# A decoder layer on one core: inverse roots of the norms moved from VectorE to GpSimd

## The reference

```python
def l2norm(x):
    return x * jax.lax.rsqrt(jnp.sum(x * x, -1, keepdims=True) + 1e-06)      # on q and k, per head
...
def head_stats(x):
    mean = x.mean(-1)
    var = ((x - mean[..., None]) ** 2).mean(-1)
    am = jnp.abs(x).mean(-1)
    l2 = jnp.sqrt((x * x).sum(-1))
    return jnp.stack([mean, var, am, l2], -1).mean(2)
def rmsnorm(x, w):
    return x * jax.lax.rsqrt((x * x).mean(-1, keepdims=True) + EPS) * w
...
x = _layernorm(x + _L0_attn_ref(...), axis=-1)    # delta rule, convolutions, mixture of four sources, gate
x = _layernorm(x + _L0_xattn_ref(...), axis=-1)   # retention over a context
x = _layernorm(x + _L0_ffn_ref(...), axis=-1)     # eight experts, the best two of each token count
```

## Time and profile before

| | |
|---|---|
| Median of 3 runs | 513.29 us (512.7 to 514.06) |
| Span of the profiled execution, first to last instruction | 510.6 us |
| Median less that span (the profiled execution lists no time of its own beside its span) | 2.7 us |
| PE matmul busy | 401.5 us, 79% of the span |
| DVE busy | 323.2 us, 63% |
| ACT busy | 159.2 us, 31% |
| POOL busy | 39.3 us, 8%, nearly all of it before 160 us |
| DVE instructions | 1050 |

### The profile page before, as it was taken

One profiled execution on the slowest core, in us unless ns is written; L12 is line 12 of the kernel. 1 busy time (PEld: TensorE's weight loads), 2 busy tenths in 40 slices (PEclk: granted clock), 3 DMA queues, 4 the chain that ended last, 5 costly groups with the idle time before them and its releaser, 6 DMA issues.

```text
span 510.6 us, 8321 instructions
## 1 busy us (share of the span) xinstructions
PE 401.5 (79%) x2952; PEld 293.4 (57%) x2952; DVE 323.2 (63%) x1050; ACT 159.2 (31%) x267; POOL 39.3 (8%) x77
## 2 busy tenths in 40 slices
PE   1979999788973699984245689897998979887992
PEld 0647677467962699971023355565656546564672
DVE  2043464677999823368763576676897588777635
ACT  1252523512345211142021124422433244413430
POOL 7000000002980000000000000000000000000000
PEclk9989999997997555575555969999899989999997
DMA  7460201039653900000000000000020000000000
GB/s 246 105 186 1 42 0 22 1 75 296 166 145 88 119 3 3 3 2 0 1 1 27 15 21 1 0 22 0 2 62 2 21 0 21 0 0 1 22 2 21
DMA packets 48305, 22.23 MB, mean 44 GB/s; under 512 B 17768, under 2 KB 47632, under 8 KB 48016
## 3 DMA queue, kind: packets, MB, share of 16 engines
q1 hardware_dynamic: 31760, 13.40, 10.9%
q10 hardware_dynamic: 16512, 8.39, 6.0%
HBM read 18.64 MB, written 3.15 MB: 43 GB/s over the span
## 4 chain that ended last, share of the span: by engine, by line
PE 49%; DVE 31%; issue 9%; DMA 5%; ACT 3%; SPq 2%; DVEq 0%; ACTq 0%; POOL 0%
PE bank L460 9%; PE bank L493 5%; PE bank L691 5%; PE bank L699 5%; PE bank L721 5%; PE bank L733 4%; PE bank L442 4%; DVE prod L1430 3%; DVE inv L1432 3%; DVE as_t L1410 2%; DVE as_t L1232 2%; DVE nt L1143 2%; DVE nt L1142 2%; DVE as_t L1223 2%; DVE sm L1144 2%
## 5 line engine op out<-in xcount | busy, mean ns | idle before, releaser
L699 PEld LDWEIGHTS bank<-w_sb,as_t 128*128 128x128 f32 x512 | 61.0, 194 | 23.0 <-issue 18.8
L699 PE MATMUL bank<-w_sb,as_t 128*128 128x128 f32 x512 | 63.9, 280 | 5.0 <-ACT as_t L1002 5.0
L1002 ACT ACTIVATE as_t<-bank,cb 128x512 f32<-128x512 f32 x64 | 43.4, 687 | 76.0 <-PE bank L691 60.8
L691 PE MATMUL bank<-as_t,w_sb 128*128 128x512 f32 x128 | 66.5, 648 | 0.0
L1410 DVE SCALAR_TENSOR_TENSOR as_t<-bank,as_t 128x128 f32<-128x128 f32 x128 | 36.0, 344 | 23.4 <-PE bank L699 21.1
L460 PE MATMUL bank<-wtap,xc_pad 128*128 128x384 f32 x128 | 47.0, 514 | 3.8 <-DVE wtap L1157 3.8
L721 PE MATMUL bank<-vb,early 32*32 32x32 f32 x512 | 29.9, 236 | 11.7 <-DMA early<-inverses 11.7
L442 PE MATMUL bank<-ident,as_t 128*128 128x128 f32 (+1 forms) x64 | 12.1, 319 | 33.8 <-DVE as_t L1232 15.7
L1201 DVE TENSOR_TENSOR as_t<-bank,masks 128x512 f32 (+1 forms) x32 | 21.3, 690 | 26.7 <-PE bank L493 26.7
L460 PEld LDWEIGHTS bank<-wtap,xc_pad 128*128 128x128 f32 x128 | 25.0, 202 | 20.3 <-issue 4.3
L721 PEld LDWEIGHTS bank<-vb,early 32*32 32x32 f32 x512 | 28.2, 151 | 13.1 <-issue 12.3
(11 more groups left out here) (221 smaller groups left out, 647.5 us busy)
## 6 DMA issues: line engine op xcount, KB each, us to landing
toep<-taps_long ACTq DMA_DIRECT2D x8, 1024.0 KB, 7.0
toep<-x SPq DMA_DIRECT2D x8, 256.0 KB, 2.8
early<-x SPq DMA_DIRECT2D x4, 256.0 KB, 4.6
w_sb<-w SPq DMA_DIRECT2D x1, 1024.0 KB
w_sb<-w SPq DMA_DIRECT2D x2, 512.0 KB
blocks<-as_t SPq DMA_DIRECT2D x16, 64.0 KB, 2.0
early<-blocks SPq DMA_DIRECT2D x1, 1024.0 KB, 4.9
toep<-ctx_in SPq DMA_DIRECT2D x4, 256.0 KB, 3.4
```

Of the source, the lines that this page charges most:

```text
L691: pe.matmul(ps[4 + half][:, :], w1_sb[:, e, half * 128:half * 128 + 128], x2_c.rearrange("p b t -> p (b t)"), start=True, stop=True).then_ ...
L699: last = pe.matmul(bank(6 + e % 2)[:, b, :], hid[:, e % 2, half, b * L:(b + 1) * L], w2_sb[:, e, half, :], start=(half == 0), stop=(half = ...
L1002: act.activation(hid[:, e % 2, half, :], ps[4 + half][:, :], ACT.Relu, bias=c_of("b1", 2 * e + half)).then_inc(s["hid_ready"], 1)
```

## The change

The function `inverse_root` on POOL takes the root as one operation: the input to the power of -0.5, the exponent from a constant tile `minus_half` that POOL fills at the start. DVE asks by a semaphore `root_asked` and waits for `root_taken` (`pool_root`). Both engines count the requests in the same order, so POOL's stream names every root of every step. The roots in `norms`, `layernorm`, `mixture_stats` and `gated` are moved. Those in `source_moments` stay on DVE.

```diff
+        minus_half = sb("minus_half", [128, 2 * G * H])
...
             pool.memset(flip[:, :], 0.0).then_inc(pool_step, 1)
-            pool.wait_ge(pool_step, 12)
+            pool.memset(minus_half[:, :], -0.5).then_inc(pool_step, 1)
+            pool.wait_ge(pool_step, 13)
...
+            def inverse_root(y, a, n, asked):
+
+                pool.wait_ge(s["root_asked"], asked)
+                pool.tensor_tensor(out=y, in0=a, in1=minus_half[:, 0:n], op=ALU.pow).then_inc(s["root_taken"], 1)
+
             with pool.Fori(0, NG) as g:
                 pool.wait_ge(s["silu_ready"], (g + 1) * G)
                 pool.tensor_copy(src[:, bass.ds(g * G, G), 3, :], qkv_g[:, :, 2 * D:3 * D]).then_inc(s["v_kept"], 1)
+                inverse_root(rn_g[:, :, :].rearrange("p b h -> p (b h)"), ss_g[:, :, :].rearrange("p b h -> p (b h)"),
+                             G * 2 * H, g + 1)
...
+            def norm_root(asked):
+                inverse_root(sm2[:, 0:G], sm1[:, 0:G], G, asked)
+
+            def mixture_root(asked):
+                inverse_root(nt2[:, 0:G * H], sm2[:, 0:G * H], G * H, asked)
+
+            def gated_root(asked):
+                inverse_root(sm2[:, 0:G * H], ogr.rearrange("p b h -> p (b h)"), G * H, asked)
+
             pool.wait_ge(s["stats_ready"], 4)
             stats_of(0)
+            mixture_root(NG + 1)
+            gated_root(NG + 2)
+            norm_root(NG + 3)
             pool.wait_ge(s["stats_ready"], 5)
-            with pool.Fori(1, NG) as g:
+            stats_of(1)
+            norm_root(NG + 4)
+            mixture_root(NG + 5)
+            gated_root(NG + 6)
+            norm_root(NG + 7)
+            with pool.Fori(2, NG) as g:
                 stats_of(g)
+                norm_root(g * 5 + NG - 2)
+                norm_root(g * 5 + NG - 1)
+                mixture_root(g * 5 + NG)
+                gated_root(g * 5 + NG + 1)
+                norm_root(g * 5 + NG + 2)
+            norm_root(NG * 5 + NG - 2)
+            norm_root(NG * 5 + NG - 1)
+            norm_root(NG * 5 + NG)
...
+            roots = [0, 0]
+
+            def pool_root():
+
+                roots[1] += 1
+                dve.sem_inc(s["root_asked"], 1)
+                dve.wait_ge(s["root_taken"], roots[0] + roots[1])
...
                 own(dve.tensor_scalar(ss_g[:, :, :], ss_g[:, :, :], 1e-6, None, ALU.add))
-                rsqrt(rn_g[:, :, :].rearrange("p b h -> p (b h)"), ss_g[:, :, :].rearrange("p b h -> p (b h)"),
-                      G * 2 * H)
+                pool_root()
...
                 own(dve.tensor_scalar(sm1[:, 0:G], mv[:, :, 1], EPS, None, ALU.add))
-                rsqrt(sm2[:, 0:G], sm1[:, 0:G], G)
+                pool_root()
...
-                rsqrt(nt2[:, mine], sm2[:, mine], n * H)
+                if in_steps:
+                    pool_root()
+                else:
+                    rsqrt(nt2[:, mine], sm2[:, mine], n * H)
...
                 own(dve.tensor_scalar(ogr, ogr, 1.0 / DH, EPS, ALU.mult, ALU.add))
-                rsqrt(sm2[:, 0:G * H], ogr.rearrange("p b h -> p (b h)"), G * H)
+                pool_root()
```

More of the change, by code:

```diff
@@ L244, in decoder_kernel @@
                  "x2t_ps x2c_ready route_ps rmax_ready rexp_ready score_ready scoret_ps scoret_ready binit_ps hid_ps "
-                 "hid_ready y_ps sum_started y_added fin_ready").split()
+                 "hid_ready y_ps sum_started y_added fin_ready "
+                 "root_asked root_taken").split()
         s = {n: sem(n) for n in names}
@@ L419, in _ @@
             pool.memset(st2, 0.0).then_inc(pool_step, 1)
-            pool.wait_ge(pool_step, 15)
+            pool.wait_ge(pool_step, 16)
             def stats_of(g):
@@ L445, in _ @@
             pe.wait_ge(s["ident_ready"], 1)
-            pe.wait_ge(pool_step, 13)
+            pe.wait_ge(pool_step, 14)
             def x_transposed(g):
@@ L862, in toeplitz @@
                 act.dma_start(toep[:, k % 2, :, :], source).then_inc(toep_in[k % 2], 16)
-            act.wait_ge(pool_step, 13)
+            act.wait_ge(pool_step, 14)
             def xc_columns(g):
@@ L1206, in _ @@
             norms(0)
-            PROJ_STEPS = 13
+            PROJ_STEPS = 3
             start = base[1]
@@ L1210, in _ @@
                 base[0], base[1] = start + (g - 1) * PROJ_STEPS, 0
+                roots[0], roots[1] = g, 0
                 mask_products(g - 1, 0)
@@ L1216, in _ @@
             base[0], base[1] = 0, start + (NG - 1) * PROJ_STEPS
+            roots[0], roots[1] = 0, NG
             for r in range(2):
@@ L1247, in head_sums, with head_moments @@
                                   axis=AX.X, op=ALU.add)
-            def head_moments(to, n, first=0):
+            def head_moments(to, n, first=0, in_steps=False):
                 mine = slice(first * H, (first + n) * H)
@@ L1328, in mixture_stats @@
                 head_sums(o_g, sq_g[:, 0:G, :], lambda k: st2[:, :, k], G)
-                head_moments(lambda k: st2[:, :, k], G)
+                head_moments(lambda k: st2[:, :, k], G, 0, True)
                 dve.tensor_tensor(out=st2[:, :, 0:4], in0=st2[:, :, 0:4], in1=mid(stat_scale[:, 0:4], G),
@@ L1472, in _ @@
                 source_sums(2, g * G, g * G + G, 4 + g)
-            dve.wait_ge(pool_step, 15)
+            dve.wait_ge(pool_step, 16)
             dve.wait_ge(w_late, 16 * LATE_LOADS)
@@ L1514, in _ @@
             step(1, False)
-            MIX_STEPS = 101
+            assert roots[1] == NG + 7, roots[1]
+            MIX_STEPS = 51
             start = base[1]
@@ L1518, in _ @@
                 base[0], base[1] = start + (g - 2) * MIX_STEPS, 0
+                roots[0], roots[1] = g * 5 + NG - 3, 0
                 step(g, True)
@@ L1521, in _ @@
             base[0], base[1] = 0, start + (NG - 2) * MIX_STEPS
+            roots[0], roots[1] = 0, NG * 5 + NG - 3
             p, q = NG - 1, NG - 2
```

## The result

The changed kernel takes 519.76 us (median of 4 runs, 518.69 to 520.97), the kernel before 513.0 (4 runs, 512.67 to 514.06): a ratio of 1.0136, 95% interval 1.0111 to 1.0161. It is 6.8 us slower where 11 us less were forecast; of the rivals, the first two ("the power is dear by the column" and "every root costs a like amount above 2 us") have the right sign. The profiled execution of the changed kernel has a span of 517.0 us, 6.4 more than before.

What follows compares the result with a forecast made beforehand. PE's waits for DVE were taken as the bound: 15.7 us before layer norms' transposes, 6.1 before the gates'. Terms -0.2, 1.3, 1.8, 3.7 and 4.6 summed to 11.2: 513.3 - 11.2 = 502 us, likeliest case 495 to 509, wider range 495 to 527.

Steps and rivals of the forecast that it cites:

- the power is dear by the column: Rival: arithmetic inside the one POOL instruction; slower from 0.13 us a column, 531 us at 0.2; 30% shared with like-amount rival.
- every root costs a like amount above 2 us: Rival: dispatch rather than columns sets each root's cost; 10.3 us slower, 524 us; 30% shared with the dear-by-column rival.
- the price of the power by the column: Cost of the power on POOL: 0.06 us a column plus 0.2 fixed, so 0.44, 1.16, 2.12 us for 4, 16, 32 columns.
- The signals: DVE to POOL and back around each root: 0.3 us taken for both ways.
- the four-column root pays: Layer norms' twelve 4-column roots: 1.24 us gained each; 3.7 us from three with nothing in front, 4.6 from six others.
- `norms`: Four 32-column roots: groups 0 to 2 covered (1.9 us at group 0), group 3 on the path, a loss of 0.2 us.
- Nothing, PE's work hides them: Mixture's roots of groups 1 to 3 and the other `finish`: no gain counted; 5.6 us more if that cover were gone.
- The gain is swallowed: Rival: PE's waits do not shrink, held by scalar-engine work or PE's order; only 5 us gained, 508 us; chance 12%.
- PE's clock could give more: Fast end: shorter waits may spare low clock in the expert's matmuls in two steps, 3.4 us, towards 495 us.
- The first-use stall: Rival: about 6 us at POOL's first root, costing some 4 of the 11 us, 506 us; left out, chance 5%.

## Why the prediction was wrong

- **The step that failed is the price of the power by the column**, "some twenty passes over each column, 0.06 us a column". It is 0.158, above the 0.13 that the text gave as the point from which the kernel is slower. I had no row for it and placed it by a count of arithmetic that was my own choice. The rival put there worked out 531 us at 0.2; at 0.158 the bookkeeping gives 6.0 us slower, and 6.8 were measured. That it comes so near is in part luck, since the same prices missed the kernels with 16 and with 32 columns alone by 8.5 and 7 us. The run with a product in place of the power shows it: 27 us between them, and nothing else changed but the numbers that flow.
- **The signals** were right: 0.3 us taken, 0.17 measured. So was "the four-column root pays": 0.83 us each where 1.24 were forecast, 7.4 us for the twelve.
- **`norms`** with its cover of 1.9 us was right in form: 1.4 late at group 0 by the cover, measured 1.6; 7.5 in all, measured 7.2 at the last keys. The sum had it at 0.2.
- **"Nothing, PE's work hides them"** for the mixture's roots was wrong. I read that PE's matmuls ended just as the transposes started and took PE for the one that was waited for. DVE's signal came within 0.1 us of it. Where two engines end level, PE hides a gain and has no cover for a loss. Alone, the mixture roots cost 6.3 us and not 1, by the profile mostly through low clock behind the waits (5.5 us), for which the sum had no term.
- **The rival "every root above 2 us by dispatch"** falls: 0.375 us are fixed. **"The gain is swallowed"** falls with the product kernel (20.5 us faster); that PE's clock could give more was right, and more than I had allowed: in windows of 3 us that kernel's clock is at 0.97 or more from 303 to 489 us, where the kernel before has eight windows below it. **The first-use stall** was not seen: the first power took 5.45 us, the mean is 5.44, and it started 0.14 us after DVE's operation ended.
- **Single edits do not add**, even with the code in three blocks: -7.4, 9.9 and 9.2 add to 11.7, and all at once are 6.8. I can show where low clock follows a longer wait, but not why a given combination escapes it, nor how much of the 4.9 us is clock and how much are waits that the edits share; that stays open.

## What to carry to other kernels

Ask of an instruction that replaces ten what it does per element on the engine it moves to, and, without a row for it, measure it alone before counting on it: by the rows measured here the power on GpSimd pays up to about nine columns ((2.0 - 0.375 - 0.17) / 0.158, an estimate, since only 4, 16 and 32 were run), so the better kernel moves only the twelve 4-column roots, 506.4 us. Where PE and the engine that feeds it end within 0.1 us of each other, count gains as hidden and losses as exposed, and expect a stretch of low clock behind a new wait on top. And before explaining a difference in a loop whose instructions did not change, count the packets of code: adding or removing instructions anywhere ahead moves the loop over its blocks.

## What the runs showed of the hardware that was not expected

- The power on GpSimd: 0.375 us and 0.158 us a column of 128 partitions, at 4, 16 and 32 columns alike; a product 0.20 to 0.25 us at the same sizes. GpSimd was free and the signals cheap; its arithmetic was the cost.
- A loop of 293 to 329 instructions on VectorE is loaded again in its second pass, with a stall of 3.2 to 3.5 us, when it touches four 8-KB blocks of code, and not when it touches three. 32 idle instructions took 5 us off one kernel, 90 put 4.5 on another. The six kernels placed anew after the rule was found all came out as it says (in the one of 4 and 16 columns the loop lies at 544 to 781, 11 packets).
- TensorE's granted clock fell to 0.5 (1.2 of 2.4 GHz) after a wait of 2.56 us between two stretches of matmuls that had run at full clock, and what followed took 1.8 times as long. After an idle stretch of 9.49 us in the projection it was 0.50 to 0.55 for 6 us of matmuls, which cost 2.7 us on top of the wait.
